# Layer weights and h of a three-round graph network kernel in float16 halves, three products in place of one float32 product

## What is computed

```
h = relu(layernorm(x))
agg_src  = segment_sum(h[src], dst);  agg_edge = segment_sum(edge_attr, dst)
x = x + relu(concat(h, agg_src, agg_edge) @ W.T + b)
h = relu(layernorm(x))
h1  = relu(mean_over_edges(h[src]) @ W1_l + b1 + h @ W1_r)
out = relu(mean_over_edges(h1[src]) @ W2_l + b2 + h1 @ W2_r)
x = x + out
```

## Time and profile before

| | us |
|---|---|
| median of 3 runs | 2005.73 (2001.06 to 2007.51) |
| profiled execution | 2020.07 |
| its span, first to last instruction | 2018.4 |

### The profile page before, as it was taken

How to read it: one execution, slowest core, us unless ns; L and a number is a source line. 1 busy time by engine, 2 the same in 40 slices (tenths; PEclk the granted TensorE clock), 3 DMA queues, 4 the chain that set the end, 5 groups by cost and what they waited for, 6 DMA issues and landing times.

```text
span 2018.4 us, 34734 instructions
## 1 busy us (share of the span) xinstructions
PE 1504.6 (75%) x12154; PEld 1267.0 (63%) x12155; DVE 808.6 (40%) x1830; ACT 492.8 (24%) x1399; POOL 636.8 (32%) x772
## 2 busy tenths in 40 slices
PE   3769999999999437777668916667768816776678
PEld 3659999999999325655457704556557604554457
DVE  8469988888888002332224301111112201110012
ACT  3421345688888001111112200000001000000000
POOL 4200011112212643334530272433540373335430
PEclk8779999999999757888788957778878957787779
DMA  4057888899989413332333423333343413344433
GB/s 131 22 149 206 229 242 245 261 270 268 278 264 278 144 49 101 135 121 95 111 88 141 144 53 97 130 103 118 112 130 119 134 52 126 116 125 137 109 118 95
DMA packets 284761, 295.11 MB, mean 146 GB/s; under 512 B 19461, under 2 KB 250064, under 8 KB 284672
## 3 DMA queue, kind: packets, MB, share of 16 engines
q1 hardware_dynamic: 233861, 212.90, 34.1%
q0 software_dynamic: 26016, 69.24, 12.2%
q10 hardware_dynamic: 24795, 11.74, 2.0%
HBM read 245.70 MB, written 48.11 MB: 146 GB/s over the span
## 4 chain that ended last, share of the span: by engine, by line
PE 69%; issue 17%; another core or an unknown queue 8%; DVE 3%; ACT 2%; DMA 0%; ACTq 0%; SPq 0%; DVEq 0%; POOL 0%; POOLq 0%
PE edge_banks L1091 35%; PE edge_banks L1049 15%; PE banks L1023 7%; PE edge_banks L1122 3%; PE edge_banks L1045 3%; PE banks L1109 3%; PE banks L911 1%; PE banks L1103 1%; ACT own L1222 1%; PE edge_banks L1098 1%; DVE edge_t L1430 0%; ACT shared L1279 0%; DMA shared<-in_dst 0%; DVE shared L1397 0%
## 5 line engine op out<-in xcount | busy, mean ns | idle before, releaser
L847 POOL DMA_INDIRECT shared<-g_rows,list_src x555 | 523.8, 944 | 767.8 <-PE edge_banks L1122 448.8
L1091 PE MATMUL edge_banks<-g_even,shared 128*128 128x257 f16 (+1 forms) x3822 | 532.7, 291 | 247.7 <-issue 242.7
L1091 PEld LDWEIGHTS edge_banks<-g_even,shared 128*128 128x128 fp8e3 x3822 | 390.3, 103 | 375.3 <-issue 304.5
L1049 PE MATMUL edge_banks<-shared 128*128 128x128 f32 x2744 | 344.9, 276 | 5.2 <-issue 5.1
L1091 PE MATMUL edge_banks<-shared 128*128 128x256 f16 x1911 | 265.7, 289 | 91.1 <-issue 90.4
L1049 PEld LDWEIGHTS edge_banks<-shared 128*128 128x128 f32 x2744 | 325.1, 192 | 8.9 <-issue 8.2
L1663 DVE SCALAR_TENSOR_TENSOR shared<-edge_banks,shared,own 128x128 f32<-128x128 f32 x98 | 34.3, 350 | 739.5 <-PE edge_banks L1091 433.7
L1091 PEld LDWEIGHTS edge_banks<-shared 128*128 128x128 fp8e3 x1911 | 195.2, 103 | 151.3 <-issue 114.5
L826 POOL DMA_DIRECT2D counts<-shared x156 | 76.4, 490 | 481.5 <-ACT shared L1279 466.6
L1575 DVE TENSOR_TENSOR shared<-iota,shared 128x3528 f16<-128x3528 f16 x98 | 195.4, 1994 | 36.6 <-PE banks L1023 35.5
L1279 ACT ACTIVATE shared<-banks 128x392 uint16<-128x392 f32 x312 | 152.0, 487 | 176.9 <-PE banks L1023 166.9
(11 more groups left out here) (282 smaller groups left out, 1069.9 us busy)
## 6 DMA issues: line engine op xcount, KB each, us to landing
shared<-in_edge_attr SPq DMA_DIRECT2D x195, 512.0 KB, 4.6
shared<-counts SPq DMA_DIRECT2D x117, 784.0 KB
counts<-shared POOLq DMA_DIRECT2D x156, 196.0 KB, 4.0
shared<-g_rows,list_src POOLq DMA_INDIRECT x555
shared<-hot_rows SPq DMA_DIRECT2D x20, 304.0 KB
g_rows<-g_even SPq DMA_DIRECT2D x1, 3136.0 KB, 15.5
g_rows<-shared ACTq DMA_DIRECT2D x49, 64.0 KB
g_rows<-g_even ACTq DMA_DIRECT2D x49, 64.0 KB
```

What stands on the lines that cost most here:

```text
L847: pool.indirect_dma_start(ring_g[use % RING][:, t, 0:2 * D], None, g_rows[r], bass.IndirectOffsetOnAxis(ap=list_src[:, at:at + 1], axis=0) ...
L1049: mm = pe.matmul(edge_wide[bank][:, :, at], ring[:, bank * GROUP_TILES + j, :], hot_dst[u][:, k, (j - 1) * SPREAD:j * SPREAD].unsqueeze(1) ...
L1091: mm = pe.matmul(acc[s][:, 0:wide], stream8[slot][:, order[h], :], G[r % 2][:, order[h], 0:wide], start=h == 0, stop=h == BLOCKS - 1, skip ...
```

## The change

h and the four layer weights are each split into a float16 high half and a float16 rest. For h, `h16` holds both side by side; TensorE turns each by a float16 product with an identity (`turn16`), ScalarE copies 256 columns of PSUM to `hT16` in place of 128, and `dense` does three float16 products into one place in PSUM: high by high, low by high, high by low. In round 0 h is no longer written by ScalarE but by three steps of VectorE; the square root is scaled so that h comes out 1024 times as large. In round 1 a second VectorE step writes the rest. `own` now takes a scale. The weights are split once, in `split_weights`, on VectorE before round 0, in space that the build phase no longer needs; TensorE waits for it before block 1 of round 0. At the start a fifth matrix norm is taken. `w_conv`, `x` and the results stay float32, and round 2 is unchanged but for the scales it takes.

```diff
-                            pe.transpose(turn_ps[o], h_blk[:, o, :], ident[:, :]).then_inc(R["turned"], 1)
+                            for k in range(2):
+                                mm = pe.matmul(turn_ps[o][:, k * D:(k + 1) * D], h16[:, o, k * D:(k + 1) * D], turn16, start=True, stop=True)
+                            mm.then_inc(R["turned"], 1)
...
-                            pe.matmul(g_ps[o], hT_blk[:, o, :], w_conv[:, 2 * to - 2:2 * to, :].rearrange("p k f -> p (k f)"),
-                                      start=True, stop=True).then_inc(R["g_up"], 1)
+                            high, low = hT16[:, o, 0:D], hT16[:, o, D:2 * D]
+                            pe.matmul(g_ps[o], high, w_high[:, to - 1, :], start=True, stop=False, skip_group_check=True)
+                            pe.matmul(g_ps[o], low, w_high[:, to - 1, :], start=False, stop=False, skip_group_check=True)
+                            pe.matmul(g_ps[o], high, w_low[:, to - 1, :], start=False, stop=True, skip_group_check=True).then_inc(R["g_up"], 1)
...
+                        if r == 0 and i == 1:
+                            pe.wait_ge(S["w_edge_ready"], 2)
...
-            for k, w in enumerate((w_in[:, 1, :], w_conv[:, 0, :], w_conv[:, 1, :], w_conv[:, 2, :])):
+            for k, w in enumerate((w_in[:, 1, :], w_conv[:, 0, :], w_conv[:, 1, :], w_conv[:, 2, :], w_conv[:, 3, :])):
...
-                            act.activation(hT_blk[:, o, :], turn_ps[o], ACT.Copy).then_inc(R["hT_done"], 1)
+                            act.activation(hT16[:, o, :], turn_ps[o], ACT.Copy).then_inc(R["hT_done"], 1)
...
-                            act.activation(tiny[:, s, 0:1], agg_blk[:, s, 1:2], ACT.Sqrt, bias=eps).then_inc(R["std"], 1)
-                            act.wait_ge(R["norm"], n + 1)
-                            act.wait_ge(R["turned"], n + 1)
-                            act.activation(h_blk[:, s, :], x_sb[:, bs, :].rearrange("p a f -> p (a f)"), ACT.Relu,
-                                           bias=tiny[:, s, 2:3], scale=tiny[:, s, 1:2]).then_inc(R["h_done"], 1)
+                            act.activation(tiny[:, s, 0:1], agg_blk[:, s, 1:2], ACT.Sqrt, bias=eps_unit, scale=1.0 / (H_UNIT * H_UNIT)).then_inc(R["std"], 1)
...
+            def split_weights():
+                dve.wait_ge(count_stored[1], 16 * PIECES * (DENSE // 2))
+                dve.tensor_copy(turn16, ident)
...
+                for k in range(2):
+                    ins = dve.tensor_scalar(w_high[:, k, :], both[k], grow[:, k:k + 1], None, ALU.mult)
+                link(ins)
+                for k in range(2):
+                    dve.scalar_tensor_tensor(out=w_low[:, k, :], in0=both[k], scalar=grow[:, k:k + 1], in1=w_high[:, k, :], op0=ALU.mult, op1=ALU.subtract)
...
+                dve.sem_inc(S["w_edge_ready"], 1)
...
-                    dve.tensor_tensor(own[:, bs, :].rearrange("p a f -> p (a f)"), g_ps[s][:, D:2 * D], bias_all[:, r + 1, :], ALU.add
-                                      ).then_inc(R["g_done"], 1)
+                    dve.scalar_tensor_tensor(out=own[:, bs, :].rearrange("p a f -> p (a f)"), in0=g_ps[s][:, D:2 * D], scalar=own_scale[:, r:r + 1],
+                                             in1=bias_mid if r == 0 else bias_all[:, 2, :], op0=ALU.mult, op1=ALU.add).then_inc(R["g_done"], 1)
...
+                            link(dve.tensor_scalar(h_raw, a_x, tiny[:, s, 1:2], tiny[:, s, 2:3], ALU.mult, ALU.add))
+                            dve.wait_ge(R["turned"], n + 1)
+                            link(dve.tensor_scalar(h16[:, s, 0:D], h_raw, 0.0, None, ALU.max))
+                            dve.scalar_tensor_tensor(out=h16[:, s, D:2 * D], in0=h_raw, scalar=0.0, in1=h16[:, s, 0:D], op0=ALU.max, op1=ALU.subtract
+                                                     ).then_inc(R["h_done"], 1)
                         elif r == 1:
                             dve.wait_ge(R["turned"], n + 1)
-                            dve.tensor_scalar(h_blk[:, s, :], mixed_blk, 0.0, None, ALU.max).then_inc(R["h_done"], 1)
+                            link(dve.tensor_scalar(h16[:, s, 0:D], mixed_blk, 0.0, None, ALU.max))
+                            dve.scalar_tensor_tensor(out=h16[:, s, D:2 * D], in0=mixed_blk, scalar=0.0, in1=h16[:, s, 0:D], op0=ALU.max, op1=ALU.subtract
+                                                     ).then_inc(R["h_done"], 1)
```

More of the change, by code:

```diff
@@ L195, in message_passing @@
         tsum, mixed_blk = place(t0, D), place(t0 + D, D)
-        h_blk = place(t0 + 2 * D, 2 * D).rearrange("p (s f) -> p s f", f=D)
-        hT_blk = place(t0 + 4 * D, 2 * D).rearrange("p (s f) -> p s f", f=D)
+        h16 = place(t0 + 2 * D, 2 * D).bitcast(F16).rearrange("p (s f) -> p s f", f=2 * D)
+        hT16 = place(t0 + 4 * D, 2 * D).bitcast(F16).rearrange("p (s f) -> p s f", f=2 * D)
+        w1 = 12596 + 1568
+        w_high, w_low = (place(w1 + k * 2 * D, 2 * D).bitcast(F16).rearrange("p (r f) -> p r f", f=2 * D) for k in range(2))
+        turn16 = place(w1 + 4 * D, D // 2).bitcast(F16)
+        h_raw = place(w1 + 5 * D, D)
+        bias_mid = place(w1 + 6 * D, D)
+        sizes, shrink, grow = (place(w1 + 7 * D + 4 * k, 3) for k in range(3))
+        g_scale, own_scale, mid_back = (place(w1 + 7 * D + 12 + 4 * k, 2) for k in range(3))
         edge_blk = place(t0 + 6 * D, 2 * D).rearrange("p (s f) -> p s f", f=D)
@@ L310, in message_passing @@
         acc = flat[0:2]
-        turn_ps = [banks[:, i, 0:D] for i in range(2)]
+        turn_ps = [banks[:, i, 0:2 * D] for i in range(2)]
         g_ps = [banks[:, 2 + i, 0:2 * D] for i in range(2)]
@@ L887, in _ @@
             pe.wait_ge(S["squares_ready"], 1)
-            pe.matmul(flat[3][:, 0:4], ones[:, :], norms[:, 0:4], start=True, stop=True).then_inc(S["squares_up"], 1)
+            pe.matmul(flat[3][:, 0:5], ones[:, :], norms[:, 0:5], start=True, stop=True).then_inc(S["squares_up"], 1)
             pe.wait_ge(S["diff_ready"], 1)
@@ L1709, in rounds @@
                         for k in range(1, 3):
[L1710 removed]
+                            ins = dve.tensor_scalar(inv_deg[:, k, 0:BLOCKS], inv_deg[:, 0, 0:BLOCKS], mid_back[:, 0:1] if k == 1 else back[:, k:k + 1], None, ALU.mult)
                         ins.then_inc(S["inv_ready"], 1)
```

36 lines of the change are left out of this document (28 added, 8 removed).

## The result

The changed kernel takes 2020.89 us (median of 5 runs, 2016.91 to 2029.81) against 2005.73 for the kernel before: a ratio of 1.0081, 95% interval 1.0061 to 1.0101. That is 15 to 16 us slower. It lies outside the range on record (1994 to 2012), on the side to which the least chance was given.

The account below looks back on a forecast made before the run. It took TensorE's matmuls (69% of the chain) as the bound, with POOL's gathers setting window lengths. Terms -5.3 - 3.4 + 0.2 + 4.4 + 0.6 + 0.95 + 0.85 = -1.7 us took 2005.7 to 2004.0 us; range 1994 to 2012.

Parts of the forecast that it names:

- Dense product: Outside gather windows, three float16 matmuls take 0.33 us for 0.43 at full clock; gains 5.3 us, and 3.4 at half clock.
- Turn: Outside gather windows, 59 turns become two float16 matmuls taking 0.112 us for 0.11: +0.2 us, between -1.8 and +3.6.
- Instructions in windows: In gather windows of rounds 0 and 1, a fixed number of instructions passes, so extra pairs push sums out: +4.4 us.
- the first rival: Windows not limited by a count, so dense products save everywhere and extra pairs are free: -9.8 us, 1996 us; chance 0.23.
- h in round 0, behind the list block: Ten turns at the tenth sum stall 0.2 to 0.3 us for h, seven of them in windows: +0.6 us.
- The copy on ScalarE: Transpose back, 256 columns in place of 128, takes 0.38 us and stays hidden before the dense product.
- h in round 0, behind a window: Behind three windows the turn already waits for h, so the longer chain shows: +0.95 us with the one of round 1.
- The other rivals: VectorE steps holding up gathers (2021 us, 0.07); dense product not shorter (2013 us, 0.08 shared with another slow case).
- the second rival: VectorE's new steps hold up POOL's gathers in windows of rounds 0 and 1: 17 us more, 2021 us; chance 0.07.
- Splitting the weights: Before round 0, some 17 VectorE instructions, about 5 us, covered by VectorE's idle time: zero, without that cover 5 us.

Follow-up runs that it names:

- `x5_after`: The changed kernel, unedited, on a chip where the kernel before takes 1436.79 us: 1433.84 us, ratio 0.9982.
- x16: The kernel before, unedited, run again for a trace on a chip with gather windows: 2001.82 us, ratio 1.0001.
- x17: The changed kernel with round 0 back to float32, halves in round 1 only, chip with windows: 2003.44 us, ratio 1.0012 to the kernel before.
- x18: The kernel before plus a load and 8-column matmul ahead of every turn and dense product of rounds 0 and 1, chip with windows: 2026.44 us, ratio 1.0134.
- x14: The changed kernel with h made by one activation in round 0 and its low half left out, chip with windows: 2033.13 us, ratio 1.0072 to the kernel before.
- x15: The kernel before with only VectorE's longer chain for h, float32 turns and products kept, chip with windows: 2038.50 us, ratio 1.0098.
- x9: The kernel before with TensorE's sums and VectorE's first step made to wait for issued gathers, chip with windows: 2033.32 us, ratio 1.0164.

## Why the prediction was wrong, point by point

**What bounds the kernel.** That the windows matter, and that their length is POOL's, held: gathers stay 1.25 us apart whatever the kernel, but for the stops told below, and 19 of them take 23.7 us. What failed is the next step, that TensorE's instructions are all that a window costs. I treated a window as a stretch that lets through some number of instructions, read from the earlier trace rows; its effect on signals between engines had no place in the sum. The row was there to be seen: VectorE's wait "remote", 19.74 us, and, in the trace of before, a copy on ScalarE 4.1 to 6.3 us behind its turn.

**Dense product.** Right. Timeline of an ordinary block of round 0 in `x5_after`; the differences of the starts are the prices:

```profile
705.34 0.35 DVE L1722 TENSOR_SCALAR shared<-x_sb,shared 128x128 f32<-128x128 f32 x1
...
706.44 0.27 PE L1115 MATMUL banks<-shared 128*128 128x128 f16 x2
706.55 0.44 PE L1109 MATMUL edge_banks<-shared 128*128 128x128 f32 x2
...
706.75 0.38 ACT L1324 ACTIVATE shared<-banks 128x256 f16<-128x256 f32 x1 [2.46 <-PE banks L1115]
706.83 1.05 PE L1102 MATMUL edge_banks<-g_even,shared 128*128 128x257 f16 x8
...
707.72 0.27 PE L1123 MATMUL banks<-shared 128*128 128x256 f16 x1
...
707.94 0.27 PE L1125 MATMUL banks<-shared 128*128 128x256 f16 x1
708.05 4.18 PE L1102 MATMUL edge_banks<-g_even,shared 128*128 128x257 f16 x36
```

Three products take 708.05 - 707.72 = 0.33 us, as forecast. Blocks of round 1 went from 5.94 to 5.84 us.

**Turn.** The pair takes 706.55 - 706.44 = 0.11 us, 0.056 a piece, as forecast; the 81 ns that the Trainium skill gives (TensorE: Matmul & The Clock Gate, Back-to-back issue gap) is too much for this pair. But the edge product behind it takes 0.28 us to the next sum where it took 0.22: 0.06 us that no step had. Ordinary blocks of round 0 are therefore 6.19 us, not 6.13, and round 0 keeps 0.04 us of the 0.10 a block.

**Instructions in windows.** The count held and the term, +4.4 us, was too small. Matmuls that TensorE starts from the first gather to the end of the last, in the seven windows of a round (in brackets the sums with count matrices among them):

| trace | round 0 | round 1 | round 2 |
|---|---|---|---|
| before, first trace | 606 (547) | 609 (560) | 627 |
| the change, first trace | 622 (534) | 635 (551) | 662 |
| before, x16 | 631 (569) | 631 (582) | 656 |
| halves in round 1 alone, x17 | 641 (576) | 633 (549) | 653 |
| tiny pairs, x18 | 631 (543) | 646 (562) | 661 |

The first two rows look like the first rival, more instructions let through when more are there. But round 2, where the kernels do the same, rises most of all: it is the traces that differ. On one chip, x16 against x17, the windows of round 1 let 631 and 633 through, and 33 sums are pushed out behind them by 35 more instructions of turns and products. That is 3.6 us at 0.11 us each and 7 us at the 0.21 us of the half clock just behind a window, an estimate; the prediction had 39 pairs at 0.11 us for both rounds together, with a float32 pair weighing 1.3, which these counts don't bear out. What round 1 lacks is of that size: alone it gives +2 us [0, +5] with windows and -5 without.

**h in round 0, behind the list block.** The place was right, ten turns at the tenth sum, and the size about right where it can be seen: 1.6 to 1.8 us over six waits in round 0, and 3.5 us for moving the turn, of which its waits are 1.3, against 0.6 us forecast for three of the ten turns and the other seven taken as free in windows. The first step of h, which I priced like L1684 at 0.227 us, takes 0.35 in that block. The copy on ScalarE takes 0.38 us, as forecast.

**h in round 0, behind a window.** This is the step that failed most: "behind three windows the turn already waits for h", +0.95 us with the round change. The term took the moment at which VectorE starts as given and added only the longer chain. It is that moment that moves, by 2.4 us between the first two traces (23.2 to 25.6) and by 6 to 7 against `x16_before_again`, and the turn with it by 1.6 to 4.1 us in six windows, some 10 to 25 us. For the waits at the turn, priced at 0.95 us here and 0.6 us behind list blocks, the traces show 1.0 us in all before and 12.7 us with the change; 1.6 us of these are there without windows too. Sums pushed out of windows, above, are the second term that was too small. TensorE also stays longer at the half clock behind the window: the sum of matmuls' busy time in round 0 rises from 327.8 to 334.6 us while the same change lowers it from 271.3 to 270.4 us where there are no windows.

**The other rivals.** VectorE's steps of the change don't hold up gathers: beside its float32 steps they are 1.25 us apart, as without them. But another VectorE step does, and the first pair's traces happen not to show it: the making of the list table, 2.68 us, float16 to uint8. In `x16_before_again` it meets a gather in two windows:

```profile
971.83 2.68 DVE L1695 TENSOR_TENSOR shared<-iota,norm_t 128x2432 uint8<-128x2432 f16 x1
971.92 3.41 POOL L847 DMA_INDIRECT shared<-g_rows,list_src  x1 [0.30 <-issue]
975.64 0.94 POOL L847 DMA_INDIRECT shared<-g_rows,list_src  x1 [0.30 <-issue]
```

The gather takes 3.41 us in place of 0.94, and the next starts 1.12 us behind the table's end; these two windows last 25.9 and 25.7 us, not 23.4. On the chips without windows it happens nine times in round 0, with and without the change, and the next gather starts 1.12 to 1.14 us behind the table's end each time. It explains none of the 16 us, but the second rival's mechanism exists in this kernel. The lock between VectorE and GpSimd that the Trainium skill describes (SBUF — State Buffer, "SBUF: two separate sides") also holds for a VectorE step with two inputs in SBUF against a GpSimd one that reads SBUF. The table's step has two such inputs and the gather reads its row numbers from SBUF, so these traces fit it; the change's steps of 0.23 to 0.35 us show nothing of it.

The three products are as short as the sums. Splitting the weights costs nothing that can be seen: it runs on VectorE from 663.1 to 667.0 us, when TensorE has just begun its first block (666.45). The sum of the first rival takes 1.8 us where the forecast's same terms come to 2.4, which moves it by 0.6 us.

**What stays open.** Why some chips have windows. And what sets the delay of a signal within one: the turn's is longer with two more TensorE instructions (x14), with a later turn at the tenth sum and more VectorE steps (x15) and with waits alone (x9, 8.9 us), all on other chips than x16's 4.5 us; on x16's chip tiny pairs (x18) leave it at 4.8 us and raise only the later one. How the 16 us divide between the sums pushed out of windows and the late h isn't shown either.

## What to carry to other kernels

Where an engine is slow because of something outside its own work, don't price a change there in its instructions alone: follow each signal that has to get out of that stretch, and ask how near it is to its latest possible moment. A stall with a ceiling behaves like a switch, so parts measured alone may each cost the whole, as here. And where counts of two traces are compared, count a stretch too that the change leaves alone. And a pair timed on one chip is a result about that chip: the same change gains 0.2% on one chip and loses 0.7 to 0.8% on two others. The halves in round 1 alone gain 0.4% on a chip without windows and nothing on one with them; the change with the turn moved from the 10th to the 14th sum gains 0.4% without windows and wasn't tried with them. No version was shown to be faster on both kinds.

## What was not expected of the hardware

The same kernel takes 1437 us on two chips and 2000 to 2020 us on the others, with the same gather spacing of 1.25 us. On the first kind TensorE runs at the full clock beside the gathers, with 257.50 us busy of 257.50. On the second it stops again and again, often for 0.7, 1.4, 2.1 or 2.8 us, and a signal from it takes 3 to 10 us to reach ScalarE (turn to copy) and 7 to 16 us to reach VectorE (last sum of the block to VectorE's step). A pair of a load and an 8-column matmul costs 0.06 us ahead of the turn and 0.11 us ahead of the dense product, where a 128-column float16 pair in the turn costs 0.056 us. A float32 product behind a float16 pair costs 0.06 us more than behind a float32 one. And a VectorE step of 2.68 us that meets a gather holds it until its own end.
